# A transformer block on one core: the attention's second product moved behind the next tile's scores

## The reference

```
sigs = levels 1..4 of the path signature, running products and sums over time
h    = sigs @ tok_W.T + tok_b                                   # 4096 tokens x 128
x    = layernorm(h)
q, k, v = split(x @ Wq.T)          # 8 heads of 64, Wq, Wo normed by one power iteration
attn = softmax(q k' * exp(temperature), own position masked)
h    = h + (attn v) @ Wo.T + b_out
x2   = layernorm(h)
e    = argmax(x2 @ gate_w.T)                                    # one of 8 experts
h    = h + w2[e] (silu(w1[e] x2) * w3[e] x2) + sw2 gelu(sw1 x2) # expert and shared FFN
```

## Time and profile before

| | us |
|---|---|
| runs (3) | 715.45, 715.73, 715.82; median 715.73 |
| profiled execution, its own time | 715.07 |
| its span | 713.1 |
| busy in the span: PE, PEld | 664.4 (93%), 512.9 (72%) |
| busy: DVE, ACT, POOL | 436.7 (61%), 297.4 (42%), 334.1 (47%) |
| mean granted TensorE clock | 0.977 of full speed |

### The profile page before, as it was taken

The page is one execution under the profiler, slowest core; times in us unless marked ns, Lnnn a source line. Parts: engine busy times, 40 slices in busy tenths (PEclk is TensorE's granted clock), DMA queues, the critical chain, the costliest instruction groups (busy, mean ns, idle before and its releaser), DMA issues.

```text
span 713.1 us, 13737 instructions
## 1 busy us (share of the span) xinstructions
PE 664.4 (93%) x3976; PEld 512.9 (72%) x3977; DVE 436.7 (61%) x1085; ACT 297.4 (42%) x701; POOL 334.1 (47%) x344
## 2 busy tenths in 40 slices
PE   4789999999999999999999999998879769999993
PEld 1567777777778777877777777876769737777772
DVE  6676776767766776767676776765374125445441
ACT  3314444454435444454435444443746124434440
POOL 5765453454435453455445443541027704544553
PEclk9799999999999999999999999999899979999998
DMA  8915221112211211112111211121244222323230
GB/s 329 171 64 203 49 47 33 37 34 61 63 37 33 58 37 37 33 44 52 33 37 33 63 33 37 33 56 41 66 173 136 75 56 40 42 39 41 38 41 5
DMA packets 40847, 45.28 MB, mean 63 GB/s; under 512 B 6272, under 2 KB 29184, under 8 KB 40448
## 3 DMA queue, kind: packets, MB, share of 16 engines
q1 hardware_dynamic: 34192, 40.86, 21.5%
q0 software_dynamic: 6640, 4.22, 4.3%
HBM read 17.30 MB, written 11.44 MB: 40 GB/s over the span
## 4 chain that ended last, share of the span: by engine, by line
PE 79%; POOL 8%; DVE 5%; issue 5%; DMA 1%; ACT 1%; SPq 0%; POOLq 0%; DVEq 0%
PE bank L1112 69%; POOL sorted_rows L523 4%; PE bank L1375 3%; PE bank L1271 2%; PE bank L1159 2%; PE bank L1251 1%; POOL e L432 1%; POOL e3l L444 1%; PE bank L1358 1%; POOL g L440 1%; POOL z L449 1%; DMA sq<-square 0%; PE bank L1193 0%; PE bank L1202 0%; DVE h L744 0%
## 5 line engine op out<-in xcount | busy, mean ns | idle before, releaser
L1112 PE MATMUL bank<-whigh,uth 128*128 128x512 f32 x512 | 168.4, 410 | 0.8 <-DVE lowt L740 0.8
L449 POOL TENSOR_TENSOR z<-z 128x512 f32<-128x512 f32 x32 | 40.8, 1276 | 182.3 <-DVE z L824 182.3
L1112 PEld LDWEIGHTS bank<-whigh,uth 128*128 128x128 f32 x512 | 89.8, 190 | 40.6 <-issue 25.5
L1112 PE MATMUL bank<-whigh,utl 128*128 128x512 f32 x256 | 100.9, 394 | 0.0
L531 POOL DMA_INDIRECT out<-z,ids x39 | 60.8, 1558 | 73.3 <-ACT z L703 73.0
L458 POOL TENSOR_TENSOR rstd<-rstd,powers 128x1 f32<-128x1 f32 x64 | 35.3, 552 | 71.3 <-DVE rstd L841 49.8
L1112 PE MATMUL bank<-xT,qkw 128*128 128x128 f32 x512 | 64.0, 279 | 0.0
L1085 DVE COPY xvp<-bank 128x512 f32<-128x512 f32 x39 | 27.0, 692 | 60.0 <-PE bank L1375 60.0
L562 ACT CAST uth<-bank 128x512 fp32r<-128x512 f32 x32 | 18.8, 586 | 105.6 <-PE bank L1164 105.6
L1112 PEld LDWEIGHTS bank<-xT,qkw 128*128 128x128 f32 x512 | 61.3, 196 | 0.1
L1112 PEld LDWEIGHTS bank<-whigh,utl 128*128 128x128 f32 x256 | 48.3, 189 | 11.2
(11 more groups left out here) (206 smaller groups left out, 1481.0 us busy)
## 6 DMA issues: line engine op xcount, KB each, us to landing
xvp<-xvo SPq DMA_DIRECT2D x128, 128.0 KB, 2.3
w<-w_t SPq DMA_DIRECT2D x1, 4096.0 KB, 13.4
sorted_rows<-x SPq DMA_DIRECT2D x3, 838.5 KB, 14.7
prob<-sorted_rows SPq DMA_DIRECT2D x39, 64.5 KB, 1.8
w<-w_high SPq DMA_DIRECT2D x4, 512.0 KB, 5.4
x_columns<-x2t SPq DMA_DIRECT2D x32, 64.0 KB, 1.6
xg_in<-x_columns SPq DMA_DIRECT2D x8, 256.0 KB, 3.2
levels<-w_t SPq DMA_DIRECT2D x1, 2048.0 KB, 8.6
```

The source lines that it names most:

```text
L449: G.tensor_tensor(z4[:], z[:, 0:4, :], z[:, 4:8, :], ALU.add).then_inc(tree, 1)
L1112: return T.matmul(out_, lhsT, rhs, start=start, stop=stop)
```

## The change

The second product becomes `values(t)`. In iteration i TensorE runs `values(i-1)` right behind the scores of tile i. The residual, the second norm and x2n of tile i-1 follow in iteration i on VectorE, the columns of x2n now at the end of the turn, and the router of tile i-2 behind the score weights of tile i. Semaphore waits and the written-out tiles at both ends are adapted (`older` is false in the first turn with a tile before it).

```diff
@@ GpSimd, iteration(i, f, u, acc, prev=True) @@
                 if f:
                     level3_rest(i + 3)
+                if prev:
+                    root(1, ln2, i - 1)
                 if u:
                     add_channels(i + 2)
-                root(1, ln2, i)
@@ ScalarE, iteration(i, f, acc, prev=True, older=True) @@
-                if prev:
-                    keep_x2(i - 1)
+                if prev and older:
+                    keep_x2(i - 2)
...
             iteration(TILES - 1, False, False)
+            keep_x2(TILES - 2)
             keep_x2(TILES - 1)
             x2_transposed(TILES - 1)
@@ VectorE, iteration(i, f, u, acc, prev=True, older=True) @@
+                if prev and older:
+                    keep_logits(i - 2)
...
+                if prev:
+                    residual(i - 1)
                 if acc:
                     x_lo(i + 1)
+                if prev:
+                    finish = second_norm(i - 1, not older)
                 if u:
                     weigh(i + 2, 0)
                 if f:
                     level4(i + 3)
                 if prev:
-                    keep_logits(i - 1)
-                residual(i)
+                    finish()
                 if u:
                     weigh(i + 2, 1)
-                finish = second_norm(i, not prev)
                 if f:
                     features_lo(i + 3)
-                finish()
...
             iteration(TILES - 1, False, False, False)
+            residual(TILES - 1)
+            finish = second_norm(TILES - 1)
+            finish()
+            keep_logits(TILES - 2)
             keep_logits(TILES - 1)
@@ TensorE @@
+            def values(t):
+
+                pe.wait_ge(xv_moved, 64 * t + 64)
+                pe.wait_ge(pT_sb, t + 1)
+                for c in range(PAIRS):
+                    for s in range(2):
+                        last = mm(B[7][col(s, LEN), 0:DIM], pt[:, c, s, :], xvp[:, s, c, :],
+                                  c == 0, c == PAIRS - 1)
+                last.then_inc(att_psum, 1)
@@ TensorE, iteration(i, f, u, acc, prev=True, older=True) @@
+                if prev and older:
+                    router(i - 2)
                 pe.wait_ge(xT_lo, i + 1)
-                if prev:
-                    pe.wait_ge(h2_done, i)
+                if prev and older:
+                    pe.wait_ge(h2_done, i - 1)
...
                 last.then_inc(s_psum, 1)
+                pe.wait_ge(vo_sb, 2 * i + 1)
+                if prev:
+                    values(i - 1)
                 if u:
                     project(i + 2, 1, 5)
...
                 last.then_inc(p_psum, 1)
-                if prev:
-                    x2_columns(i - 1)
                 if u:
                     project(i + 2, 8, 9)
                 if f:
                     sum_level3(i + 3)
                 if is_tile(i, LAST):
                     down(0, 0, range(1), True)
-                pe.wait_ge(vo_sb, 2 * i + 2)
-                pe.wait_ge(xv_moved, 64 * i + 64)
-                pe.wait_ge(pT_sb, i + 1)
...
+                    pe.wait_ge(h2_done, TILES - 1)
+                    values(TILES - 1)
+                if u:
+                    project(i + 2, 9, 10)
                 if prev:
-                    router(i - 1)
+                    x2_columns(i - 1)
                 if is_tile(i, LAST):
                     down(0, 0, range(1, GROUP), True)
-                if u:
-                    project(i + 2, 9, 10)
+                    router(TILES - 2)
                 if f:
                     features(i + 3)
```

More of the change, by code:

```diff
@@ L459, in root, with iteration @@
                     .then_inc(rooted[n], 1)
-            def iteration(i, f, u, acc):
+            def iteration(i, f, u, acc, prev=True):
                 if f:
@@ L509, in _ @@
             add_channels(1)
-            with pool.Fori(0, TILES - 3) as i:
+            iteration(0, True, True, True, False)
+            with pool.Fori(1, TILES - 3) as i:
                 iteration(i, True, True, True)
@@ L514, in _ @@
             iteration(TILES - 1, False, False, False)
+            root(1, ln2, TILES - 1)
             nc.gpsimd.iota(x2[:, :, DIM:ROW].bitcast(I32), pattern=[[P, TILES], [1, 1]], base=0,
@@ L578, in keep_x2, with iteration @@
                 A.copy(x2[:, bass.ds(t, 1), 0:DIM].rearrange("p o d -> p (o d)"), x2n[:]).then_inc(x2_kept, 1)
-            def iteration(i, f, acc, prev=True, second=False):
+            def iteration(i, f, acc, prev=True, older=True):
                 for n in range(2):
@@ L609, in iteration @@
                 if prev:
-                    x2_transposed(i - 1, second)
+                    x2_transposed(i - 1, not older)
                 if f:
@@ L651, in _ @@
             A.copy(sw1[:, 0, :], sw1_in).then_inc(sw_hi, 1)
-            iteration(1, True, True, True, True)
+            iteration(1, True, True, True, False)
             with a.Fori(2, TILES - 3) as i:
@@ L883, in x_group_lo, with iteration @@
                 remainder(xgl[k], xg_in[:, k, :], xgh[k], xg_lo)
-            def iteration(i, f, u, acc, prev=True):
+            def iteration(i, f, u, acc, prev=True, older=True):
+                if prev and older:
+                    keep_logits(i - 2)
                 if is_tile(i, LAST_BUT_ONE):
@@ L992, in _ @@
             remainder(sw1[:, 1, :], sw1_in, sw1[:, 0, :], sw_lo)
-            with d.Fori(1, TILES - 3) as i:
+            iteration(1, True, True, True, True, False)
+            with d.Fori(2, TILES - 3) as i:
                 iteration(i, True, True, True)
@@ L1233, in iteration @@
                     pe.wait_ge(vo_sb, 2 * i)
+                    pe.wait_ge(pT_sb, i)
                 for hd in range(HEADS):
@@ L1249, in iteration @@
                 pe.wait_ge(g_sb, 2 * i + 2)
+                if prev and older:
+                    pe.wait_ge(lg_sb, i - 1)
                 T.matmul(B[4][:], ident_b[:], mask[:], start=True, stop=False)
@@ L1326, in _ @@
             iteration(0, True, True, True, False)
-            with pe.Fori(1, TILES - 3) as i:
+            iteration(1, True, True, True, True, False)
+            with pe.Fori(2, TILES - 3) as i:
                 iteration(i, True, True, True)
```

## The result

The changed kernel takes **727.72 us** (median of four executions, 726.22 to 729.08). In the same comparison the kernel before takes 715.59. The ratio is 1.0174, 95% interval 1.0145 to 1.0204: the change costs 12 us. The profiled execution is the one of 728.79 us; its span is 727.0, that of before 713.1, so this pair of profiles differs by 13.9.

A forecast was written before the change was run, and what follows sets the result against it. TensorE bounds the loop, so every wait is paid once per tile; behind it the last tile's chain counts. Stage terms sum to +15.2 on 715.07, so 730.3, as median 730.9 us; range 723 to 739.

The forecast's parts named there:

- The stall: In the loop, TensorE waits before the transposes of u, because u and x2n come late: 0.80 us per tile.
- The choice of 0.35 over 1.08 for x2n: VectorE's x2n in its new place takes 0.35 us; the rival of 1.08 gave 751.3 us, chance 0.04.
- the signs that the prediction named: Loop: 28 or 29 waits for x2n, about 0.7 us each, turns of 15.05; end: statistics 5.2 us behind probabilities.
- The saving: Second product right behind the scores saves entering and leaving the 64-column shape: 0.25 us for each of 31 products.
- +14.9: Loop term, tiles 2 to 28: 27 turns, each 0.55 us longer (stall 0.80 less saving 0.25).
- Tile 1: Start of the loop: a loop turn's +0.55 us, less 0.2 for the missing router: +0.3.
- Tiles 30 and 31: Up to tile 31's probabilities: between 1.6 us won and, if Gelus take that back, +0.5; taken as -0.7.
- The tail: Behind tile 31's probabilities: second norm waits for tile 30's x2n store, starting 5.2 us behind, not 3.65: +1.6 us.
- Only u is late: Rival, in the loop: x2n ready before u, stall 0.53 us, net +0.28 per tile; 723.4 us, chance 0.05.
- The gain alone: Rival, in the loop: x2n and u come in time, only the saving counts; -7.7, 708.0 us, chance 0.07.
- The clock did not fall in the loop: Rival: the wait drops TensorE's granted clock once in each of 28 turns, 1.6 us each; 776 us, chance 0.03.
- The total: Whole kernel: all stages sum to +15.2 us, 730.3 for the profiled execution, 730.9 as median; forecast's chance 0.79.

The follow-up runs named there:

- e2: Changed kernel with the level-3 sums (e3h, e3l) moved in front of the last whigh products on TensorE; 707.98 us, ratio 0.9904.
- e8: Changed kernel with three unread products added on GpSimd behind the second norm's root; 755.15 us on the second chip, ratio 1.0272.
- e4: Changed kernel with two whigh products and one utl put between scores and second product; 739.04 us, ratio 1.0339.
- e3: Changed kernel with x2n made before u on VectorE and the level-3 sums before the last whigh products on TensorE; 703.60 us, ratio 0.9842.
- e1: Changed kernel with x2n made before u on VectorE; 719.44 us, ratio 1.0063.
- e9: The changed kernel itself, unedited, measured again on the third chip; 727.96 us, ratio 1.0176.
- e5: Changed kernel with only its end mended: tile 30's x2n stored before the Gelus, logits kept earlier, router earlier; 747.52 us on the second chip, ratio 1.0154.
- e6: Changed kernel with the edits of e3 and e5 together; 722.59 us on the second chip, ratio 0.9818.
- e7: e6 with tile 29's x2n columns, router and copy into x2t moved from tile 30 into tile 31; 721.17 us on the second chip, ratio 0.9803.

## Why the prediction was right or wrong

- **The sign, the place and the cause** were right. TensorE was full in the loop, so a wait there is paid once a tile; the wait is the one for x2n in front of its transpose, since the products that covered u had been moved away. e2 shows this from the other side: put cover back, and the loss is gone.
- **The stall**, step by step: u 0.43 behind e3l (0.44 measured), x2n 0.35 long (0.34), transposes of u 1.60 behind e3l (1.60). The choice of 0.35 over 1.08 for x2n was right, and e8 gives the reason: it turns on what GpSimd does at that moment. The whole cost of the wait is 0.86, not 0.80. Of the signs that the prediction named, the waits came out at 0.58 in the list, not 0.7.
- **The saving was sized too small**: 0.25 against 0.36. The parts that the sum counted do make 0.25, but not as it divided them. The step into the shape falls away (0.33 to 0.23 us), the step out of it falls away behind the scores (1.01 to 0.91), and the second product's own 16 passes go from 1.02 to 0.97 or 0.98 and not to 0.9, since TensorE still leaves the shape behind them. Left out was the pair behind, which takes 0.56 behind a 64-column group and 0.46 elsewhere (e4): 0.09 here. The row was there, 314.02 to 314.82 with router and wlow in it, but the sum took it as the router's and wlow's own cost. The router gives the last 0.02: it took 0.24 and now adds 0.22, as the first products of vow stand 1.71 us behind the score weights' start in the kernel before,

```profile
302.67 0.71 PE L1112 MATMUL bank<-vow,xTh 128*128 128x512 f32 x2
```

  and 1.93 behind it in e3 (307.33 to 309.26). Tile 29, which has no level 3 and so no wait, shows the saving in the changed kernel itself: -0.39. Saving 0.11 too small and wait 0.06 too small make the turn 0.05 too long, over 27 turns +1.4 of the +14.9.
- The Trainium skill says that changing the tiling mode drains TensorE (TensorEngine Tiling (Array Packing), Key Properties). The measurements agree that a change costs time, 0.36 to 0.39 us for one entry and exit with what they do to their neighbours; that this time is a drain, no row shows. The rule alone would still have given the wrong sign, since it sees only the products that move and not what they covered.
- **Tile 1** was taken as a loop turn less its router. But before, it was longer than one (14.90). A wait for xn stood in it, listed at 0.16 us; from the start of the wlow products in front of xn's transpose to the whigh products behind it, it took 0.87, in a turn of the loop 0.50. With the change that wait is gone: -0.19 in place of +0.3.
- **Tiles 30 and 31**: -0.7 predicted, -1.74 measured. 1.46 of it lies where the prediction looked: tile 31's turn starts 2.55 us behind tile 30's probabilities, before 4.01. That is the bound at which the Gelus take nothing back (4.0 - 2.4 = 1.6), and the step that failed was to go near the middle between the two bounds. Another 0.3 us fell away in tile 30 in front of its probabilities, which the sum had at nothing.
- **The tail**: +1.6 predicted, +2.8 measured. The mechanism held (the store behind two Gelus and a cast), at 4.91 us, not 5.2. What was not foreseen stands behind it: the granted clock falls in the middle of the up products,

```profile
512.60:516.00 3.40, 3.19 (x15) 3.19 (x16) 0.43 (x2) 2.65 (x5) 0.00 (x0) 0.50 0.06 19
533.10:536.50 3.40, 3.40 (x9) 2.65 (x8) 1.43 (x4) 1.35 (x3) 0.00 (x0) 0.50 0.86 357
```

  The columns are those of the earlier trace rows. The first window, in tile 30, answers to the one there; the second is new, and all of its 3.40 us TensorE worked at 1.2 GHz on up products. In front of it TensorE had stood idle for 1.20 us and, after 1.2 us of work, for 0.86; in e3 it stands idle in the same places for the same times, and the clock does not fall, so what decides it is open. The fall makes 1.54 of the +2.8, the later store the other 1.27, and the runs part the two. e2 and e3 have the same end as the changed kernel and make tile 31's x2n at the same distance from the probabilities (6.40), but in their profiles the clock stays at 1.00 up to the scatter, and it follows 19.03 behind the probabilities, not 20.57. In the profiles of the changed kernel (both of them), of e1 and of e4, where the clock falls in this stretch, it is 20.3 to 20.6. The difference lies in one wait of VectorE, for products that stand behind the up products; in the changed kernel and in e3:

```profile
538.11 0.42 DVE L1039 COPY e<-bank 128x256 f32<-128x256 f32 x1 [3.47 <-PE bank L1124]
```

```profile
511.76 0.42 DVE L1039 COPY e<-bank 128x256 f32<-128x256 f32 x1 [1.93 <-PE bank L1124]
```

- **The rivals.** "Only u is late" was priced at a stall of 0.53; e1 is this rival made real, and its turn is 0.60 above that of e3. "The gain alone" was priced at 708.0 beside a kernel before of 715.73; e3, whose loop has the gain and no wait, takes 703.6 beside one of 714.26, though its profile also lacks the fall of the clock behind tile 31. The clock did not fall in the loop, where the granted clock is 1.0 throughout.
- **The total**: +15.2 predicted for the profiled execution, +13.7 measured (715.07 to 728.79), by median +12.1. The changed kernel's own executions spread over 2.9 us; those with a mean granted clock of 0.977 have spans of 727.0 and 727.3, those with 0.981 and 0.982 have 724.4 to 724.9. The order by clock is not strict: in e9 an execution with 0.975 has 726.2, one with 0.977 has 727.3. The profiled execution lies at the upper end. That the total came so near is in part luck: the sum had some 3 us too much in the loop, in tile 1 and in tiles 30 and 31, and 1.7 too little in the tail and at both ends.

Not tried: to move the second product and leave the second norm where it was, since the norm needs that product; why the clock falls in some executions only; what TensorE waited for on the second chip.

## What to carry to other kernels

On an engine that is full, work that looks movable may be the cover of a chain on another engine. Before moving it, count from the producer (here e3l) to the consumer (the transposes of u) how much work is left between, and if it is less than the chain takes, move the producer forward with it: here that turned +12 us into -6, and with x2n early as well into -11. Products of the same array shape belong together; keeping one group apart from the other costs 0.36 to 0.39 us here, a quarter of it in the products behind.

## What the runs showed of the hardware

- Leaving the 64-column shape costs in the next group as well: a 512-column pair takes 0.56 us behind it and 0.46 elsewhere.
- Two 8-column router passes between 128-column ones add 0.22 us (1.93 from the score weights to vow in e3, 1.71 in the kernel before), and took 0.24 us behind the second product (314.02 to 314.26 in the kernel before). Their own step reads 0.14, but the pass in front of them takes 0.08 longer: a step between two starts is no price by itself.
- x2n takes 0.34 us on VectorE with nothing beside it on GpSimd. Beside GpSimd's work it ends 0.09 us behind that, and so lasts 1.09 us in one case and 0.51 in another (e8). xn, the same operation, does the same.
- A granted clock of 0.50 over 3.40 us of up products delays the scatter by 1.54 us (20.57 against 19.03 behind the probabilities).
- The kernel before takes 714 to 716 us in three of the comparisons and 736 in the one of e5 to e8. The kernels profiled beside it there have the turns of the loop that they have elsewhere (15.00 for e5, 14.15 for e6 and e7) and 20 us more behind the loop; the cause is open.
